# Pairs of key and value tiles whose products are summed in the accumulator banks, and two more such pairs

## The reference, cut to what matters

```
qkv = relu(xn @ qkv_weight.T)            # q, k, v: 32 heads of 16
vk  = einsum('bnhe,bnhd->bhed', [v, 1], k)    # summed over the tokens of a batch
y   = (vk q)[:D] / ((vk q)[D:] + EPS) @ proj_weight.T + proj_bias
```

## Time and profile before

| | |
|---|---|
| median of 3 runs | 1869.14 us (1868.93 to 1870.22) |
| span of the profiled execution, first to last instruction | 1866.2 us |
| TensorE busy | 1835.4 us (98%) |
| VectorE busy | 1254.6 us (67%) |
| ScalarE busy | 820.8 us (44%) |
| GpSimd busy | 410.2 us (22%) |
| granted TensorE clock, mean | 0.999 |

### The profile page before, as it was taken

The page is one execution under the profiler, slowest core; times in us unless marked ns, Lnnn a source line. Parts: engine busy times, 40 slices in busy tenths (PEclk is TensorE's granted clock), DMA queues, the critical chain, the costliest instruction groups (busy, mean ns, idle before and its releaser), DMA issues. The chain is left out here.

```text
span 1866.2 us, 25384 instructions
## 1 busy us (share of the span) xinstructions
PE 1835.4 (98%) x8780; PEld 1520.1 (81%) x8780; DVE 1254.6 (67%) x2374; ACT 820.8 (44%) x1421; POOL 410.2 (22%) x467
## 2 busy tenths in 40 slices
PE   7999999999999999998999999999999999999998
PEld 6888888888788888887888788888888888888886
DVE  6555565564568888884898756666666666666666
ACT  4555555554233443333787533333333333333333
POOL 2000000000004555520000233322222222333331
PEclk9999999999999999999999999999999999999999
DMA  5653525543325444433788421222222222222211
GB/s 221 242 197 119 197 89 211 198 150 133 106 73 181 149 157 145 148 121 100 233 264 258 151 100 52 74 91 96 95 96 95 96 96 95 76 84 86 95 51 68
DMA packets 106350, 246.81 MB, mean 132 GB/s; under 512 B 30624, under 2 KB 54000, under 8 KB 98544
## 3 DMA queue, kind: packets, MB, share of 16 engines
q1 hardware_dynamic: 97952, 236.63, 35.7%
q0 software_dynamic: 8272, 8.57, 1.6%
HBM read 161.52 MB, written 83.63 MB: 131 GB/s over the span
## 5 line engine op out<-in xcount | busy, mean ns | idle before, releaser
L649 DVE TENSOR_TENSOR spl<-sp_t,sph 128x512 fp32r<-128x512 f32 x128 | 88.6, 692 | 195.2 <-ACT sph L449 195.2
L111 PE MATMUL AB_E<-xs,enc_h 128*128 128x512 f32 x512 | 207.6, 405 | 1.2 <-DVE xs L637 1.2
L1924 PE MATMUL D_D<-dec_h,rateh 128*128 128x512 f32 x512 | 200.5, 392 | 2.2 <-DVE ratel L2032 2.2
L113 PE MATMUL AB_E<-xs,enc_h 128*128 128x512 f32 x512 | 200.6, 392 | 0.0
L112 PE MATMUL AB_E<-xs,enc_l 128*128 128x512 f32 x512 | 200.2, 391 | 0.0
L1925 PE MATMUL D_D<-dec_l,rateh 128*128 128x512 f32 x512 | 199.9, 390 | 0.0
L1926 PE MATMUL D_D<-dec_h,ratel 128*128 128x512 f32 x512 | 199.4, 389 | 0.0
L445 ACT ACTIVATE sp_t<-AB_E,cols 128x512 f32<-128x512 f32 x128 | 88.2, 689 | 201.6 <-PE AB_E L113 198.8
L1075 POOL DMA_INDIRECT slots_scratch<-ctok,idx x128 | 131.8, 1030 | 191.8 <-DVE part L1393 165.8
L1767 POOL DMA_INDIRECT ga<-eo_scratch,idx x64 | 66.4, 1037 | 485.3 <-DVE ratel L2032 466.1
L1823 ACT ACTIVATE rate<-D_Y,cols 128x512 f32<-128x512 f32 x128 | 88.0, 687 | 118.0 <-PE D_Y L1905 118.0
(11 more groups left out here) (418 smaller groups left out, 4764.5 us busy)
## 6 DMA issues: line engine op xcount, KB each, us to landing
xs_scratch<-xs SPq DMA_DIRECT2D x16, 2048.0 KB, 8.9
xsd<-xs_scratch SPq DMA_DIRECT2D x15, 2048.0 KB, 7.9
xs<-xs_scratch SPq DMA_DIRECT2D x14, 2048.0 KB
wt<-ew_scratch SPq DMA_DIRECT2D x39, 513.0 KB, 3.8
xd<-in_x SPq DMA_DIRECT2D x16, 1024.0 KB, 5.3
out_y<-out SPq DMA_DIRECT2D x64, 256.0 KB, 2.0
x<-in_x SPq DMA_DIRECT2D x15, 1024.0 KB, 5.8
xf_scratch<-xt SPq DMA_DIRECT2D x12, 1024.0 KB, 8.5
```

The source lines that it names most:

```text
L111: pe.matmul(out, w_hi, x_hi, start=start, stop=False)
L113: return pe.matmul(out, w_hi, x_lo, start=False, stop=stop)
L649: dve.tensor_tensor(T["spl"][:, n % 3, :], T["sp_t"][:, m % 2, :], f32(T["sph"][:, n % 3, :]), ALU.subtract)\
L1924: pe.matmul(bD[t][:, :], rateh[:, n % 3, o], T["dec_h"][:, k, :], start=(k == 0), stop=False)
```

## The change

The pairs begin at tile 8, so there are 26 and 8 + 4 single tiles (8 at the front, 4 at the end); the front stage keeps one block of x more. Products are added in the banks: a pair has a bank x, y and z; x takes M1, then M6, M7 and M4 on top, z takes M5, then M3, and y takes M2. TensorE's order is M1, M5, M6, `outer(2q-2)`, M7, `outer(2q-1)`, M2, M3, M4. ScalarE copies out three states: M1 (`even_k`), M5 (`odd_v`) and M1 + M6 (`even_v`), each counted by `kept`. VectorE adds three times: `odd_v` += x after M7, `even_k` += y after M2, `even_v` += z after M3. The odd key is read from x itself after M4; td has the other sign for that. TensorE waits for the copy of M1 before M6, for the copy of M1 + M6 before M7 and for the addition of `odd_v` before M4; at the first pair it waits for all split weights before M5. ScalarE's rounding of S1 for the next pair stands between the second and third copy. VectorE's low part of the even value moves to the head of the next pair, in front of that of the odd key, behind the side work of the pair. The dispatch steps go 3, 3, 3, 1, 0, 0, 4, 2 to the single tiles and 2, 2 to the first two pairs, behind the sums of x. The weight sums start a tile number 3 (4 before), the splits go by two, one and one to tiles 5 to 7, and the x sums of the first pair go to tile 5. The projection weight is still loaded at pair 8, now written Q0 + 4. Left out below: banks' names, the changed waits of single tiles, POOL's waits (now `V_ODD`, `K_EVEN`, `V_EVEN`).

```diff
@@ -50,7 +50,7 @@
 
 KV_ORDER = (14, 15, 8, 9, 10, 11, 12, 13, 1, 2, 3, 4, 5, 6, 7, 0)
 
-PAIR0, PAIR1 = 12, 60
+PAIR0, PAIR1 = 8, 60
 IN_PAIRS = sorted(KV_ORDER[PAIR0 // NT:PAIR1 // NT])
 
...
@@ -776,12 +776,12 @@
 
 RANK_AT, CLOSE_AT = 4, TT // 2
 
-PLACE_STEPS = (2, 2, 3, 3, 0, 0, 3, 2, 2, 2, 1, 0)
+PLACE_STEPS, PAIR_STEPS = (3, 3, 3, 1, 0, 0, 4, 2), (2, 2)
 
 W_T = KC + 1 + 2 * KC
 W_WP = W_T + 4
 
-T_AT, T_ORDER = 5, (3, 3, 4, 4)
+T_AT = 3
 W_DEC = W_WP + KC
 
...
@@ -938,13 +938,13 @@
         .then_inc(S[f"part_in{g % 4}"], 16)
 
 
-def product(pe, T, S, bank, left, right):
+def product(pe, T, S, bank, left, right, first):
 
     for c in range(2):
         (lh, ll), (rh, rl) = left(c), right(c)
-        pe.matmul(bank[:, :], lh, rh, start=(c == 0), stop=False)
-        pe.matmul(bank[:, :], lh, rl, start=False, stop=False)
-        k = pe.matmul(bank[:, :], ll, rh, start=False, stop=(c == 1))
+        pe.matmul(bank[:, :], lh, rh, start=(first and c == 0), stop=False, skip_group_check=not first)
+        pe.matmul(bank[:, :], lh, rl, start=False, stop=False, skip_group_check=not first)
+        k = pe.matmul(bank[:, :], ll, rh, start=False, stop=(c == 1), skip_group_check=not first)
     k.then_inc(S["mul_done"], 1)
 
 
...
@@ -1114,11 +1122,10 @@
                     act.wait_ge(S["b_consts"], 2)
                     act.activation(T["sc0"][:, 32:32 + TT, :], bX[:, :].rearrange("p (t e) -> p t e", e=NE), ACT.Copy)\
                         .then_inc(S["count_out"], 1)
-                if T_AT < n <= T_AT + 4:
-                    t = n - T_AT - 1
-                    act.wait_ge(S["t_raw"], T_ORDER[t])
-                    act.activation(T[f"t{'abcd'[t]}_h"][:, :, :], T[f"t{'abcd'[t]}_raw"][:, :, :], ACT.Copy)\
-                        .then_inc(S["wh_out"], 1)
+                if T_AT + 2 <= n <= T_AT + 3:
+                    act.wait_ge(S["t_raw"], 4)
+                    for t in ("ac", "bd")[n - T_AT - 2]:
+                        act.activation(T[f"t{t}_h"][:, :, :], T[f"t{t}_raw"][:, :, :], ACT.Copy).then_inc(S["wh_out"], 1)
                 if 20 <= n < 20 + KC:
                     c = n - 20
...
@@ -1152,12 +1159,20 @@
 
             def pair(q):
                 n = 2 * q
+                more = q + 1 < Q1
                 act.wait_ge(S["mul_done"], product_done(q, M1))
                 if q > Q0:
                     act.wait_ge(S["kl_out"], n - 1)
-                act.activation(part[0][:, :], pair_bank(q, M1)[:, :], ACT.Copy).then_inc(S["m1_out"], 1)
-                if q + 1 < Q1:
-                    act.wait_ge(S["mul_done"], product_done(q, M6))
+                act.activation(even_k[:, :], x_bank(q)[:, :], ACT.Copy).then_inc(S["kept"], 1)
+                act.wait_ge(S["mul_done"], product_done(q, M5))
+                if q > Q0:
+                    act.wait_ge(S["vl_out"], n)
+                act.activation(odd_v[:, :], z_bank()[:, :], ACT.Copy).then_inc(S["kept"], 1)
+                if more:
+                    high(q + 1, S1)
+                act.wait_ge(S["mul_done"], product_done(q, M6))
+                act.activation(even_v[:, :], x_bank(q)[:, :], ACT.Copy).then_inc(S["kept"], 1)
+                if more:
                     high(q + 1, S2)
                     act.wait_ge(S["mul_done"], product_done(q, M7))
                     high(q + 1, S3)
@@ -1165,19 +1180,15 @@
                     totals(0)
                 act.wait_ge(S["outer_done"], n)
                 act.wait_ge(S["post_out"], sum_done(q, V_ODD))
-                value(n + 1, part[3][:, :])
-                if q + 1 < Q1:
-                    act.wait_ge(S["mul_done"], product_done(q, M5))
-                    high(q + 1, S1)
+                value(n + 1, odd_v[:, :])
                 act.wait_ge(S["post_out"], sum_done(q, K_EVEN))
-                key(n, part[0][:, :])
+                key(n, even_k[:, :])
                 act.wait_ge(S["post_out"], sum_done(q, V_EVEN))
-                value(n, part[1][:, :])
-                if q + 1 < Q1:
-                    act.wait_ge(S["mul_done"], product_done(q, M3))
+                value(n, even_v[:, :])
+                if more:
                     high(q + 1, S4)
-                act.wait_ge(S["post_out"], sum_done(q, K_ODD))
-                key(n + 1, part[2][:, :])
+                act.wait_ge(S["mul_done"], product_done(q, M4))
+                key(n + 1, x_bank(q)[:, :])
                 beside(n)
                 beside(n + 1)
 
...
@@ -1277,26 +1282,41 @@
                 def weight(name, half=0):
                     return lambda c: (T[name + "_h"][:, 2 * half + c, :], T[name + "_l"][:, 2 * half + c, :])
 
-                def multiply(m, left, right, s=None):
-                    free(2 * PAIR0 + 7 * (q - Q0) + m)
-                    if s is not None:
-                        pe.wait_ge(S["sl_out"], split_done(q, s))
-                    product(pe, T, S, pair_bank(q, m), left, right)
+                def multiply(to, left, right, first=False):
+                    product(pe, T, S, to, left, right, first)
 
                 if first == 0:
                     pe.wait_ge(S[f"xsb_in{p % 2}"], 16 * (p // 2))
                 if q == Q0:
+                    single_evicted(2 * PAIR0 - 3)
+                else:
+                    pe.wait_ge(S["post_out"], sum_done(q - 1, K_EVEN))
+                multiply(x_bank(q), tile(0, 0), weight("wk", 0), first=True)
+                if q == Q0:
+                    single_evicted(2 * PAIR0 - 2)
                     pe.wait_ge(S["wl_out"], W_WP)
-                multiply(M1, tile(0, 0), weight("wk", 0))
-                multiply(M6, summed(S2), weight("tc"), S2)
+                else:
+                    pe.wait_ge(S["post_out"], sum_done(q - 1, V_EVEN))
+                pe.wait_ge(S["sl_out"], split_done(q, S1))
+                multiply(z_bank(), summed(S1), weight("ta"), first=True)
+                pe.wait_ge(S["kept"], kept(q, M1_KEPT))
+                pe.wait_ge(S["sl_out"], split_done(q, S2))
+                multiply(x_bank(q), summed(S2), weight("tc"))
                 if q > Q0:
                     outer(2 * q - 2)
-                multiply(M7, summed(S3), weight("tb"), S3)
+                pe.wait_ge(S["kept"], kept(q, U2_KEPT))
+                pe.wait_ge(S["sl_out"], split_done(q, S3))
+                multiply(x_bank(q), summed(S3), weight("tb"))
                 outer(2 * q - 1)
-                multiply(M5, summed(S1), weight("ta"), S1)
-                multiply(M2, tile(0, 1), weight("wk", 1))
-                multiply(M3, summed(S4), weight("wv", 1), S4)
-                multiply(M4, tile(1, 1), weight("td"))
+                if q == Q0:
+                    single_evicted(2 * PAIR0 - 1)
+                else:
+                    pe.wait_ge(S["kl_out"], 2 * q)
+                multiply(y_bank(q), tile(0, 1), weight("wk", 1), first=True)
+                pe.wait_ge(S["sl_out"], split_done(q, S4))
+                multiply(z_bank(), summed(S4), weight("wv", 1))
+                pe.wait_ge(S["post_out"], sum_done(q, V_ODD))
+                multiply(x_bank(q), tile(1, 1), weight("td"))
                 beside(2 * q)
                 beside(2 * q + 1)
...
@@ -1343,21 +1363,21 @@
             def weight_sums(n):
 
                 ta, tb, tc, td = (T[f"t{k}_raw"][:, :, :] for k in "abcd")
-                if n == T_AT - 1:
+                if n == T_AT:
                     dve.wait_ge(S["w_in3"], 16 * 5)
                     dve.tensor_tensor(ta, tb, ta, ALU.subtract).then_inc(S["t_raw"], 1)
                     dve.tensor_tensor(tb, tc, tb, ALU.subtract).then_inc(S["t_raw"], 1)
-                if n == T_AT:
+                if n == T_AT + 1:
                     dve.wait_ge(S["t_raw"], 2)
                     dve.tensor_tensor(tc, tc, ta, ALU.subtract).then_inc(S["t_raw"], 1)
                     dve.wait_ge(S["t_raw"], 3)
-                    dve.tensor_tensor(td, tc, td, ALU.subtract).then_inc(S["t_raw"], 1)
-                if T_AT + 1 < n <= T_AT + 5:
-                    t = n - T_AT - 2
-                    name = "t" + "abcd"[t]
-                    dve.wait_ge(S["wh_out"], W_T + t + 1)
-                    dve.tensor_tensor(T[name + "_l"][:, :, :], T[name + "_raw"][:, :, :], f32(T[name + "_h"][:, :, :]),
-                                      ALU.subtract).then_inc(S["wl_out"], 1)
+                    dve.tensor_tensor(td, td, tc, ALU.subtract).then_inc(S["t_raw"], 1)
+                if T_AT + 2 <= n <= T_AT + 4:
+                    for t in ("ac", "b", "d")[n - T_AT - 2]:
+                        name = "t" + t
+                        dve.wait_ge(S["wh_out"], W_T + "acbd".index(t) + 1)
+                        dve.tensor_tensor(T[name + "_l"][:, :, :], T[name + "_raw"][:, :, :], f32(T[name + "_h"][:, :, :]),
+                                          ALU.subtract).then_inc(S["wl_out"], 1)
 
             def beside(n):
                 if n == X_TURN:
@@ -1384,39 +1404,32 @@
```

(114 more changed lines are left out.)

## The result

The changed kernel takes 1884.49 us (median of 4 runs, 1882.93 to 1885.42) against 1869.39 us before: ratio 1.0077, interval 1.0065 to 1.0089, so it is slower by 0.8%. The forecast was 1886. The profiled execution, the slowest of the four, has a span of 1883.7 us; 1883.0 was the sum.

A forecast was written before the change was run, and what follows sets the result against it. TensorE was taken as the bound, busy 1835.4 of 1866.2 us. The terms -2.7 - 1.2 + 12.0 + 1.8 + 6.9 = +16.8 us gave a span of 1883.0, as a timed median 1886 us, range 1873 to 1892.

The forecast's parts named there:

- M7 behind four projections: Four pairs with a projection: VectorE's side work delays the odd key, so M7 waits 1.09 us each, 4.4 us.
- M7 behind the transposition: Pair with the transposition: M7 waits after the same side-work delay as behind a projection, 1.4 us.
- M7 behind two pairs of splits: Two pairs with two projection-weight splits each: M7 waits 2.39 us in each, 4.8 us.
- M7 behind the close: Pair closing the first batch: copies of totals and two closing operations delay the odd key, M7 waits 1.5 us.
- plain pairs: The other 17 pairs after the first: M7 0.09 us late in each, 0.3 in one with dispatch steps, 1.8 us.
- outer of tile 1: Front, tiles 0 and 1: four more dependent dispatch operations of 0.72 us, all on TensorE's path, 2.9 us.
- M5, first pair: First pair: M5 waits for td's low part, done behind value 7, 1.5 us.
- M7, first pair: First pair: no outer between M6 and M7, so M7 waits for the copy and its signal, 1.0 us.
- low clock: TensorE's clock after waits of some 3 us: slow matmuls thought possible, but full rate assumed, nothing in the sum.
- rival 3: Pairs: stalls drop the clock for a time, or each steady pair pays 0.3 us: +5 more, 1891 us, chance 0.10.
- All hidden: Pairs and front: VectorE always has sums ready before M6 ends, front has slack; -3.9, 1865.2 us, chance 0.08.
- Only the front: S1's rounding comes early enough, eight side-work pairs cost 0.1 us each, front costs stay: +5.4, 1874.5 us, chance 0.12.

The follow-up runs named there:

- the mended kernel with pairs from tile 12: Against the kernel before: pairs still from tile 12, its front kept, products summed in banks, S1 rounded behind the M1+M6 copy, first pair's waits changed: 1868.38 us, ratio 0.9998.
- the kernel with all mended: Against the changed kernel: S1 rounded behind the M1+M6 copy, dispatch steps redistributed, projection weight loaded one pair later, first pair's waits and outer changed: 1865.60 us.

## Why the prediction was right

It was right in its mechanism and within 1.5 us in the time; the terms were not all right, and that the time came so near is partly luck. Each against the issue starts of the trace after:

| term of the sum | forecast | measured |
|---|---|---|
| 12 matmuls | -2.7 | -2.7 |
| waits behind the weight splits | -1.2 | -1.2 |
| M7 behind four projections | +4.4 | +3.3 (4 x 0.83) |
| M7 behind the transposition | +1.4 | +1.0 |
| M7 behind two pairs of splits | +4.8 | +4.3 (2.15, 2.12) |
| M7 behind the close | +1.5 | +1.2 |
| plain pairs | +1.8 | 0 |
| outer of tile 1 | +2.9 | +2.8 (3.2, less 0.4 before) |
| outer of tile 6 | +1.5 | +1.5 |
| M5, first pair | +1.5 | +1.5 |
| M7, first pair | +1.0 | +1.0 |
| low clock | 0 | +3.2 (1.6, 1.6) |
| sum (the rounded terms make 16.9) | +16.8 | +15.9, of 16.1 in the stage |

**The M7 terms** are all 0.24 to 0.4 us too long. In the pair shown above, 0.24 of it is read off: key 0.04 earlier, key to copy 3.08 instead of 3.19, the copy 0.02 shorter, and ScalarE's signal 0.05 us instead of VectorE's 0.12, the one length for which no row of before stood. The same 0.05 us and a copy on the very edge leave plain pairs at 11.46 to 11.49 us, the period before: this term of the sum was mis-sized by all of its 1.8 us. The waits at M7 stand where they were forecast and nowhere else in the loop: there is none at M1, M2, M3, M4 or M6.

**The low clock** was priced at nothing in the sum and stood in rival 3. It happened, twice, at 1.6 us each: 3.2 us together where the rival had 5. (Each stretch holds some 13 matmuls; one of 512 columns is issued 0.20 us later there, not the 0.24 by which the rows' lengths differ.) The two errors cancel, which is luck: with the measured M7 terms alone the sum would have been +12.7, with the clock alone +20.0. That the span came within 0.7 us of the sum is luck too, as 1.4 us of it is the later first matmul. The page "TensorE: Matmul & The Clock Gate", Part 1, of the Trainium skill, which I had weighed in the prediction, says that idleness brings the array back to half rate; the windows at 0.61 and 0.50 agree. Waits alone don't decide it, though: of the two waits of 2.0 us at M7 in the changed kernel one was followed by such a stretch and one not, in the kernel with the steps put back neither was. Over the four traces with waits of 2.0 to 2.6 us at M7 it is three of eight.

**The rivals.** "All hidden" asked for the odd key to start under 1.0 us; it starts at 1.02 in plain pairs and 3.35 behind splits. "Only the front" is, in its mechanism, what the kernel with S1 moved shows: 1871.2 us, where I had put 1874.5. The waits of the front came as worked out (four rows of the table).

**What stays open.** 0.2 us of the stage. What makes the clock fall behind one wait and not behind another of the same length. Whether the low clock behind the two waits would come in each execution: the medians don't say, and the 2.3 us more that moving S1 gained may be due to it.

## What to carry to other kernels

When accumulation moves from an elementwise engine into the banks, the copies that remain become gates of TensorE: each stands in an in-order queue, and everything put ahead of it, with all that this waits for on a third engine, is then on TensorE's path. Put first into the queue what TensorE waits for soonest, and what only the next round needs behind it; here one line moved was worth 13 us, while VectorE's load of 64% had told nothing of it. And when the start of a pattern is moved forward, list the work that its old start had room for: three of the four costs at the front were this.

## What the runs showed of the hardware

The granted clock falls to half in eight of the nine traces with a changed kernel before tile 2 is done, at one of two places. In six it falls at the stage's beginning, for some 3.5 us, and costs 1.6 us of late issues in each. In the changed kernel and the one with S1 moved it falls behind the 3.2 us wait at tile 1, for 3.6 and 6 us, and costs 1.6 and 2.8. The trace of before and that of the mended kernel with pairs from tile 12 have neither. Ahead of the stage's beginning TensorE is idle twice around four small matmuls, shown here from the kernel with all mended:

```profile
485.51 0.61 PE L568 MATMUL A_L<-r,rhh 128*128 128x16 f32 x4 [1.53 <-DVE rhh L665]
486.96 0.47 PE L284 MATMUL B_KV<-wk_h,xs 128*128 128x512 f32 x1 [0.83 <-PEq L293]
```

All ten traces have these two waits, of 1.5 and 0.8 us, before's too, so the waits alone don't tell the six from the four. The changed kernel has the same code up to here as the ones with one more operation and with the sums first, and yet its clock fell in another place than theirs. So executions of one kernel probably differ by 1 to 3 us here; with one trace of each that isn't shown.

Where the stretch comes early it delays TensorE by the 1.6 us by which the wait at tile 1 is then shorter: 1.6 instead of 3.2 us in the kernel with one more operation, which starts the same. In both kernels the outer accumulation of tile 1 comes 2.9 us later after the stage's first matmul than it did before. A wait that was a queue's lateness is not added to a slow stretch ahead of it, but filled by it.
